# A deformable-convolution sampling phase: three taps by dense products instead of two, 12 gathers per step instead of 14, rows spread by DMA, clip and product fused in place

## What is computed

```python
h = relu(bn(conv2d(x, rb_w1))); h = relu(bn(conv2d(h, rb_w2)) + x)
off_out = conv2d(h, off_w) + off_b                # 2*2*9 offsets and 2*9 masks a pixel
py = offset_y + iy + ky;  px = offset_x + ix + kx # for each of 9 taps, 2 groups of channels
val = sum over the four neighbours of (py, px):   # bilinear; outside the image is 0
      h[neighbour] * weight_y * weight_x
g = val * sigmoid(mask)
out = einsum('odck,bdckhw->bohw', dc_w, g) + dc_b # 64 out, 2 groups, 32 channels, 9 taps
out = leaky(bn(out)); out = leaky(bn(conv1x1(out, cv2_w))); return x + out
```

## Time and profile before

| | |
|---|---|
| median of 3 runs | 3894.52 us (3894.42 to 3894.78) |
| the profiled execution | 3895.74 us, span 3893.8 us |
| PE / DVE / ACT / POOL busy | 81% / 79% / 75% / 23% of the span |
| mean granted TensorE clock | 0.874 |
| the sampling phase | from 2655 us to the end |

### The profile page before, as it was taken

How to read it: one execution, slowest core, us unless ns; L and a number is a source line. 1 busy time by engine, 2 the same in 40 slices (tenths; PEclk the granted TensorE clock), 3 DMA queues, 4 the chain that set the end, 5 groups by cost and what they waited for, 6 DMA issues and landing times. The chain is left out here.

```text
span 3893.8 us, 60459 instructions
## 1 busy us (share of the span) xinstructions
PE 3159.3 (81%) x23158; PEld 1237.1 (32%) x23158; DVE 3068.5 (79%) x3296; ACT 2901.4 (75%) x2963; POOL 909.1 (23%) x974
## 2 busy tenths in 40 slices
PE   4677649999999999999999999996466676776666
PEld 2455423233333333323433333332122222222212
DVE  5888667999999999599999999984466766656555
ACT  0777424999999999599999999991466656656554
POOL 0100000000000000000000000000677777777775
PEclk7677668999999999999999999998687777887677
DMA  2300000000000000000000000001213123122211
GB/s 44 109 1 1 1 3 1 1 2 2 1 1 1 2 2 1 1 1 2 1 2 1 1 2 1 1 1 29 53 53 74 53 59 74 53 66 66 59 53 43
DMA packets 117244, 89.66 MB, mean 23 GB/s; under 512 B 96496, under 2 KB 98065, under 8 KB 116957
## 3 DMA queue, kind: packets, MB, share of 16 engines
q0 software_dynamic: 28672, 58.78, 5.4%
q1 hardware_dynamic: 86652, 26.30, 3.0%
q10 hardware_dynamic: 1632, 0.56, 0.1%
HBM read 65.60 MB, written 19.96 MB: 22 GB/s over the span
## 5 line engine op out<-in xcount | busy, mean ns | idle before, releaser
L1587 ACT ACTIVATE adder_layer_Z<-adder_layer_CP,AN 128x2048 f32 x984 | 1873.7, 2009 | 37.0 <-PE PS L1534 36.2
L1534 PE MATMUL PS<-adder_layer_Z,c_adder_out 128*32 128x512 f32 x16896 | 1844.7, 593 | 62.5 <-ACT adder_layer_Z L1587 33.1
L1637 DVE TENSOR_SCALAR adder_layer_Z<-adder_layer_CP,AW 128x2048 f32 x1128 | 1370.0, 1281 | 35.4 <-PE PS L1534 31.0
L1534 PEld LDWEIGHTS PS<-adder_layer_Z,c_adder_out 128*32 128x32 f32 x16896 | 652.9, 110 | 1254.0 <-issue 1190.7
L2046 POOL DMA_INDIRECT sampler_G<-neighbours,sampler_IDX x896 | 853.6, 953 | 353.1 <-issue 272.7
L1644 DVE SCALAR_TENSOR_TENSOR adder_layer_Z<-adder_layer_CP,AW,adder_layer_Z 128x1024 f32<-128x1024 f32 x384 | 476.4, 1282 | 33.5 <-issue 33.5
L2333 ACT ACTIVATE sampler_HY<-PS,G_hat 128x512 f32<-128x512 f32 x512 | 308.5, 685 | 226.7 <-PE PS L2212 142.4
L2105 DVE TENSOR_TENSOR sampler_G<-sampler_G,PS 128x1792 f32<-128x1792 f32 x64 | 129.4, 2021 | 168.2 <-DMA sampler_G<-neighbours,sampler_IDX 163.7
L2221 PE MATMUL PS<-sampler_HXM,G_spread 32*128 32x512 f32 x128 | 97.8, 853 | 193.3 <-DVEq L2138 192.2
L2335 ACT ACTIVATE sampler_HY<-sampler_HY 128x2048 f32<-128x2048 f32 x128 | 244.5, 1910 | 9.3 <-issue 0.7
L1492 POOL MEMSET adder_layer_CP<- 128x4624 f32 x2 | 7.9, 3954 | 1023.0 <-POOLq L1487 1022.8
(11 more groups left out here) (389 smaller groups left out, 2730.0 us busy)
## 6 DMA issues: line engine op xcount, KB each, us to landing
sampler_G<-neighbours,sampler_IDX POOLq DMA_INDIRECT x896
neighbours<-top_k_zero SPq DMA_DIRECT2D x16, 578.0 KB, 7.1
neighbours<-sampler_HT SPq DMA_DIRECT2D x256, 32.0 KB, 1.7
X<-in_x SPq DMA_DIRECT2D x8, 256.0 KB, 6.2
out<-X SPq DMA_DIRECT2D x8, 256.0 KB, 3.3
P<-in_L_conv_conv_w SPq DMA_DIRECT2D x4, 144.0 KB
P<-in_L_conv_add_w SPq DMA_DIRECT2D x4, 144.0 KB
RAW<-in_L_conv_w SPq DMA_DIRECT2D x4, 144.0 KB
```

What stands on the lines that cost most here:

```text
L1534: mm = t.matmul(PS[32 * j:32 * j + 32, k, :], K["adder_out"][:, 32 * i:32 * i + 32], Z[:, r % SLOTS, j, c:c + BANK], start=False, stop=Fal ...
L1587: op = a.activation(z(r, j), seen(ch, ty, tx), ACT.Relu, bias=ANf[:, weight(ty, tx, j, i)])
L1637: op = v.tensor_scalar(z(r, j), seen(ch, ty, taps[0]), AWf[:, weight(ty, taps[0], j, i)], 0.0, ALU.subtract, ALU.max)
```

## The change

- Six taps by gathers (12 per step), three dense: 96 units, so three parts of units per step in place of two. The tables of weights change to match; the products of `deform` have three full chunks instead of four.
- The row of py is no longer spread by PE. The offsets of an image are written to DRAM (`offsets`), and SP reads a row of them into all 128 partitions of `YB` (SBUF). The x hats are copied by four SBUF-to-SBUF DMAs per unit into `HXB`, now in SBUF. SP's queue holds these spreads for all units in order; the stores of the next image are placed between them, 16 at each of units 15 to 18.
- ACT writes |py - y| into a ring of four parts `M`; the clip is done on DVE together with the product, in place. In it min(|d|, 1) * hx stands for (1 - max(0, 1 - |d|)) * hx; the sign is put into the weights `DCD`, and the missing sum over rows is added by a product with `HSUM`, the sums of the features' columns (`column_sums`, stage 7).
- For the first image 24 of the 64 stores go out on ACT's queue, right behind the copy of `HT`; the other 40 on SP, with `keep_offsets` after the first 20 of them.
- The convolutions of the stages are issued on PE in three pieces between other work; orders within a step and lags change (`LAST` 13, `FINAL` 14, two buffers for the contracted result).
- At the end of the second adder layer only the border is cleared, the clip goes image by image on DVE, and ACT copies the images into the padded one.

```diff
-NTAP = 7
+NTAP = 6
+NCHUNK = GK * CG // 128
+NUNIT = NB * HALVES * DG * NDENSE * PX // BANK
...
-                            g.memset(XP[:, :, :, :], 0.0)
+                            g.memset(XP[:, :, 0:HP:HP - 1, :], 0.0)
+                            g.memset(XP[:, :, 1:H + 1, 0:WP:WP - 1], 0.0)
...
+                        else:
+                            a.wait_ge(border, 1)
+                            for b in range(NB):
+                                a.wait_ge(normed, b + 2)
+                                a.activation(XPin[:, b], X4[:, b], ACT.Copy)
...
+            M = [HY[:, 0], HY[:, 1], spare[...], RAW2[...]]
+            YB, HXB = sb("YB", [128, 2, BANK]), sb("HXB", [128, 2, BANK])
...
+                    if b == 0:
+                        a.wait_ge(h_t, 1)
+                        for place in PLACES[0:ACT_STORES]:
+                            store(a, 0, *place)
...
+                    def keep_offsets(b):
+                        sp.wait_ge(off_sb, 2 * b + 2)
+                        sp.dma_start(offsets[b][:, :], OFF[:, b % 2]).then_inc(rows_out, 16)
+
+                    def spread(w):
+                        b, k, ti, h, d = unit(w)
+                        ch, e = channel(h, d, ti, k), w % 4
+                        sp.wait_ge(rows_out, 16 * (b + 1))
+                        if w >= 2:
+                            sp.wait_ge(hy, 2 * w - 2)
+                        sp.dma_start(YB[:, w % 2, :], offsets[b][ch:ch + 1, BANK * k:BANK * k + BANK]
+                                     .broadcast_to([128, BANK])).then_inc(y_in[w % 2], 16)
+                        sp.wait_ge(hxm, w // 4 + 1)
+                        if w >= 2:
+                            sp.wait_ge(mixed, 2 * w - 2)
+                        for yr in range(4):
+                            sp.dma_start(HXB[32 * yr:32 * yr + 32, w % 2, :], HXM[32 * e:32 * e + 32, w // 4 % 2, :])\
+                              .then_inc(x_in[w % 2], 16)
...
-                    def mix(th):
-                        v.wait_ge(hx_ps, th + 1)
-                        for part in range(2):
-                            v.wait_ge(hy, 2 * th + part + 1)
-                            if th:
-                                v.wait_ge(added, 2 * th + part - 1)
-                            v.tensor_tensor(M[part][:, :, :], HY[:, part],
-                                            HXB.unsqueeze(1).broadcast_to([128, HATS, BANK]), ALU.mult)
-                            v.drain().then_inc(mixed, 1)
+                    def mix(p):
+                        w = p // 2
+                        v.wait_ge(hy, p + 1)
+                        if p % 2 == 0:
+                            v.wait_ge(x_in[w % 2], 64 * (w // 2 + 1))
+                        v.scalar_tensor_tensor(out=M[p % 4], in0=M[p % 4], scalar=1.0,
+                                               in1=HXB[:, w % 2, :].unsqueeze(1).broadcast_to([128, HATS, BANK]),
+                                               op0=ALU.min, op1=ALU.mult)
+                        v.drain().then_inc(mixed, 1)
...
                             sample(n)
-                            if n and prepared(n - 1) is not None:
-                                mask_hats(prepared(n - 1))
+                            for p in parts(n):
+                                mix(p)
+                                if p % PARTS == 0 and prepared(n - 1) is not None:
+                                    mask_hats(prepared(n - 1))
                             next_stage(v, stage_dve, n, 1)
-                            mix(n)
...
+                    def hats(p):
+                        w, part = p // 2, p % 2
+                        if part == 0:
+                            a.wait_ge(y_in[w % 2], 16 * (w // 2 + 1))
+                        if p >= 4:
+                            a.wait_ge(added, p - 3)
+                        for j in range(HATS):
+                            c = HATS * part + j
+                            a.activation(M[p % 4][:, j, :], YB[:, w % 2, :], ACT.Abs, bias=GR["hat"][:, c:c + 1])
+                        a.drain().then_inc(hy, 1)
...
+                    def column_sums(g):
+                        b, k, ti, _, _ = unit(4 * g)
+                        if ti == 0 and g:
+                            t.wait_ge(d_sb, g // NDENSE)
+                        t.wait_ge(hxm, g + 1)
+                        t.wait_ge(h_t, 2 * b + 2)
+                        t.matmul(DB, HDC[:, ti, :], HXM[:, g % 2, :], start=(ti == 0), stop=False,
+                                 skip_group_check=True)
```

More of the change, by code:

```diff
@@ L132 @@
          "adder_x", "to_nat"]
-GRIDS = ["grid_base", "grid", "place", "hat", "spread"]
+GRIDS = ["grid_base", "grid", "place", "hat"]
 def halves(ap):
@@ L196, in program @@
     tables = [nc.dram_tensor(f"neighbours{b}", [HALVES * DG * NENT, 4 * CG], F32).ap() for b in range(NB)]
+    offsets = [nc.dram_tensor(f"offsets{b}", [128, PX], F32).ap() for b in range(NB)]
     outer = ExitStack()
@@ L1835, in stage_pe @@
                     turn(t, H2).then_inc(h_t_ps, 1)
                 elif s == 5:
-                    if b == 0:
+                    if first and b == 0:
                         t.wait_ge(w_sb, 2)
                         t.wait_ge(gridded, 16 * len(GRIDS))
[L1840 to L1844, removed]
@@ L1845, in stage_pe @@
-                    mm.then_inc(off_ps, 1)
-                elif s == 6:
+                    if first:
+                        t.wait_ge(h_t, 2 * b + 1)
+                    convolve(t, WB[2], XP[:, b], False, piece, last=False)
+                    if final:
+                        for k in range(2):
+                            mm = t.matmul(pre(k), GR["place"][:, :], half(GR["grid"], k), start=False, stop=True,
+                                          skip_group_check=True)
+                        mm.then_inc(conv_ps, 1)
+                elif s == 6 and first:
@@ L1847, in stage_pe @@
                     t.wait_ge(off_sb, 2 * b + 2)
                     turn(t, OFF[:, b % 2]).then_inc(off_t_ps, 1)
+                elif s == 7 and first:
+                    t.wait_ge(off_t, b + 1)
+                    t.wait_ge(block2, 2 * b + 2)
+                    for ti in range(NDENSE):
+                        for e in range(4):
+                            rows, c = slice(32 * e, 32 * e + 32), 128 * ti + 64 * (e // DG)
+                            mm = t.matmul(PS[rows, 6, c:c + 64], HSUM[rows, :], DCD[rows, NDENSE * (e % DG) + ti, :],
+                                          start=True, stop=True, skip_group_check=True)
+                    mm.then_inc(h_t_ps, 1)
@@ L1918, in stage_dve @@
                     v.tensor_copy(whole_image(XP[:, b]), square(H2[:, :]))
+                    v.drain().then_inc(block2, 1)
+                    v.tensor_reduce(HSUM[:, :], H2[:, :].rearrange("p (y x) -> p x y", x=W), AX.X, ALU.add)
                     v.drain().then_inc(block2, 1)
@@ new lines, in _ @@
+                    sp.wait_ge(h_t, 1)
+                    mine = PLACES[ACT_STORES:]
+                    for place in mine[0:20]:
+                        store(sp, 0, *place)
+                    keep_offsets(0)
+                    for place in mine[20:]:
+                        store(sp, 0, *place)
+                    for w in range(NUNIT):
+                        spread(w)
+                        b, u = w // (NUNIT // NB), w % (NUNIT // NB)
+                        if u == 11 and b:
@@ L2359, in _ @@
                     weigh(0)
-                    hats(0)
+                    for p in parts(0):
+                        hats(p)
                     for n in range(NT + OUTER - per_bank + 1):
@@ L2372, in _ @@
                         next_stage(a, stage_act, n, 1)
-                        if n + 1 < NT:
-                            hats(n + 1)
+                        for p in parts(n + 1):
+                            hats(p)
+                        if due(n, OUTER) is not None:
+                            finish(due(n, OUTER))
+                        if due(n, BLOCK) is not None:
+                            block(due(n, BLOCK))
         phase(sampler)
```

325 lines of the change are left out of this document (163 added, 162 removed).

## The result

The changed kernel takes 3976.7 us (median of 4 runs, 3972.9 to 3977.3) against 3894.5 before: ratio 1.0211, 95% interval 1.0197 to 1.0226. It is slower by 82 us, with 128 gathers fewer. 3986 was forecast, with 3915 to 4065 around it.

A forecast was written before the change was run, and what follows sets the result against it. POOL's gather issue was taken as the bound. 3895.74 profiled, +100 for the sampling phase, -8.5 for the start and 0 for the tail gave 3987, set to 3986 for the runs' median; range 3915 to 4065.

The forecast's parts named there:

- The bound: Sampling phase: POOL's gather issue sets the time, 1.25 us undisturbed pace; DVE, ACT and PE have slack.
- the first rival: Sampling phase: a long mix lets gathers through, POOL keeps 1.25 us, DVE close behind; 3728 us, chance 0.13.
- The hold: Gathers starting beside a two-SBUF-input DVE mix stand to its end, then need 0.82 us; three mixes cost 4.7 us.
- the slope of tensor_tensor: Mix on DVE: 1.043 ns an element, carried from 1.282 us on 1024 elements to 2.35 on 2048.
- the +0.3 for a mask multiply: Sampling phase: a mask multiply between two mixes adds 0.3 us in each of 23 steps, 7 us.
- the bare step: Sampling phase: a step without the mask-multiply addition takes 18.4 to 19.7 us, middle 19.1.
- The middle of the two phases: Sampling step: 19.1 us, between 18.4 and 19.7, depending on whether the sixth gather starts just ahead of the mix.
- The phase's sum: Sampling phase, first to last gather: 15 + 1203 + 7 = 1225 us against 1125, +100.
- The start: Before the first gather: adder layer's end 3.5 us less, stores split over ACT and SP; together -8.5 (-12 to -3).
- The tail: Last gather to output store: one mix more, no wait for hats ahead of the first; 0, between -1 and +4.
- The short hold: Sampling phase: gathers need the port only for a moment and pass during a long mix; 3728 us, chance 0.13.
- Mixes coming apart: Sampling phase: late spread rows or hats separate mixes, each meeting its own gather; 4026 us, chance 0.15.

The follow-up runs named there:

- e1: Changed kernel with the mix's second input a constant row in PSUM instead of HXB in SBUF (x hats left out); 3720.8 us.
- e4: Changed kernel with DVE copying each unit's row HXB into a free PSUM bank and mixing from there, nothing left out; 3741.7 us, ratio to before 0.9610.
- e8: Changed kernel with each mix as eight DVE instructions on 256 elements, nothing left out; 3761.0 us.
- e9: e4 with every third row copy, that of a unit that begins a step, done by ACT instead of DVE; 3745.7 us.
- e5: Kernel before the change with its tensor_tensor mix reading the row from SBUF in place of PSUM (right row left out); 4076.7 us.
- e7: Changed kernel with each mix as two DVE instructions on 1024 elements, nothing left out; 3778.9 us, ratio to before 0.9703.
- e3: Changed kernel with each mix as four DVE instructions on 512 elements, nothing left out; 3763.9 us, ratio to before 0.9665.

## Why the prediction was right

*The bound.* POOL's issue of gathers was the bound and stayed it. (The 7% of "issue" that the prediction reads stands in the page's line by engine, above the line of the earlier trace rows.) e1 shows that nothing else set the time: with the hold gone the interval is 965/767 = 1.26 us, as the earlier trace rows gave it. But DVE was close behind, as the first rival said: its waits for gathered rows fall from 357.9 us to 69.7 in e1, and in e4, e8 and e9 the chain goes through DVE.

*The hold.* The term that decided the sign had to be carried from instructions of 0.7 us to one of 2.3. It holds to the end of the instruction, and the 0.82 from that end to the gather's end is the same. The Trainium skill's rule ("SBUF — State Buffer", sections "SBUF: two separate sides" and "Who interferes with whom") that two SBUF inputs exclude a reading GpSimd instruction for the whole instruction agrees with this trace, up to 2.29 us. By the same rule of the Trainium skill a GpSimd instruction that starts first holds the DVE instruction off for its whole length; the trace doesn't show this for gathers, beside which a mix lost at most 0.07 us. The Trainium skill's other sentence there, that `tensor_tensor` did not stall descriptor generation, does not carry over to these gathers: in e5 gathers beside tensor_tensor took up to 3.03 us. Which of a gather's accesses stands still, no run here shows.

*The sizes.* The mix took 2.295 us, not 2.35; it runs as fast as the mix from PSUM (2.288), so the slope of tensor_tensor, by which 2.35 came, misled by 2%, and that of the shorter scalar_tensor_tensor rows (2.46) by 7%. The multiply took the 1754 ns of the sum, the reduction 2758 for 2793. A step came out at (1218.7 - 15)/63 = 19.1 with the mask multiplies in it, for which the sum had 7 us on top: 19.3 on average in the 23 steps with one, 19.0 in the others, so the +0.3 for a mask multiply was right and the bare step 0.1 shorter than taken. Single steps go from 18.3 to 20.6. The middle of the two phases had been taken without a count of how often each comes, so that the mean fell so near it is in part luck. The phase's sum was +93.3 for +100.

*The start* was mis-sized: -13.4 for -8.5, outside its own -12 to -3. The phase began 6.45 earlier, where I had estimated 3.5: ACT's copies take 3.90 for all four images and begin at 2644.42, ahead of DVE's last clip at 2645.18, an overlap that the estimate had not worked out. The rest is 7.0 for 5.1. A DMA on ACT took 13.23/24 = 0.55, not 0.64, and the offsets reached SP's queue at 2711.61, or 2718.1 with the 6.45 added back, for 2719.4. And the first gather came 2.1 behind the end of the last store, as in the earlier trace rows (2703.18 + 32.45 = 2735.63 to 2737.72): the 2.6 of the sum counts that store's issue a second time.

*The tail*, taken as 0 within -1 and +4, gave -2.7, also outside its range: the last mix starts 12.2 behind the last gather against 13.5, and the output store 11.6 behind that mix's start against 13.0. The three misses all go the same way, 14 us together, and the profiled execution lies 14 below the 3987 of the sum.

*The rivals.* The short hold would have given 3728, and e1 shows that this number was right for a kernel without the hold (3720.8); its condition was not met. Mixes coming apart for want of rows did not happen: no mix waited for a transfer, and the mixes of a step stand 0.1 to 0.2 behind one another, or 1.0 to 1.6 where the mask multiply lies between the first two.

## What to carry to other kernels

When a queue of software-made transfers on POOL is the bound, look at what DVE reads while it issues: here each DVE instruction with both inputs in SBUF cost the gather that met it the rest of its length. Put one input in PSUM, even at the price of a copy, or, where that can't be, cut the instruction into pieces shorter than the 1.25 us between two gathers: two, four and eight pieces left 0.95, 0.6 and 0.5 us a step of 4.0. Then look at the chain again, because the engine that pays for copies or pieces can be the next bound, as DVE was in e4 and e8. Fewer gathers do not help if what replaces them holds the others up.

## What was not expected of the hardware

Cutting an instruction in two took away three quarters of the loss, since the gathers fall in step with the ends of the pieces (0.94 and 1.01 us in e7 behind one of 1.73). The text of e7 worked this out ahead of its run; that of e3 had not seen it. A mix that met the start of a gather lost 0.07 us at most, where a gather that met a mix lost up to 2.1. And scalar_tensor_tensor of 2048 elements takes 2.295 us with both inputs in SBUF and 2.287 with one in PSUM (e1): DVE itself pays next to nothing for the place of its operand, POOL pays it.
